# Two mask instructions a batch moved from GpSimd to VectorE, and one of them written anew

## The reference

```python
x = x + L0_xattn(layernorm(x), ctx, ctx, ...)    # autocorrelation, top 12 lags
x = x + L0_ffn(layernorm(x), ...)                # 8 experts, the best one a token
x = x + L1_xattn(layernorm(x), ctx, ctx, mask, ...)
x = x + L1_ffn(layernorm(x), ...)                # ternary weights, 8-bit activations
```

```python
k = split_heads(key @ Wk.T + bk)
scores = einsum('bhqd,bhkd->bhqk', q, k) / sqrt(16)
scores = where(mask[:, None, :, :] == 0, -1e9, scores)
p = softmax(scores, axis=-1)
```

## Time and profile before

| | us |
|---|---|
| median of 3 runs | 1647.78 |
| lowest, highest | 1644.97, 1658.26 |
| profiled execution | 1647.78 |
| its span, first to last instruction | 1645.8 |
| mean granted TensorE clock (share of full) | 0.873 |

### The profile page before, as it was taken

One profiled execution on the slowest core, in us unless ns is written; L12 is line 12 of the kernel. 1 busy time (PEld: TensorE's weight loads), 2 busy tenths in 40 slices (PEclk: granted clock), 3 DMA queues, 4 the chain that ended last, 5 costly groups with the idle time before them and its releaser, 6 DMA issues.

```text
span 1645.8 us, 31869 instructions
## 1 busy us (share of the span) xinstructions
PE 1311.1 (80%) x9726; PEld 903.2 (55%) x9726; DVE 1205.0 (73%) x3428; ACT 1010.9 (61%) x2134; POOL 732.0 (44%) x890
## 2 busy tenths in 40 slices
PE   5953354788899799889888998798888988888765
PEld 4842343555666566656665666566655655555433
DVE  4773444577888788878887888788877787777743
ACT  1311221366777677767776777677766776666664
POOL 3363433245444544455445444554444444444221
PEclk9975576698999899989998999899989999888975
DMA  7762345444444444444444444444443433332100
GB/s 275 230 215 77 115 151 167 127 132 147 144 137 133 146 140 146 134 146 137 141 143 146 137 137 140 141 149 137 128 129 114 133 122 105 108 95 85 60 8 13
DMA packets 169185, 216.96 MB, mean 132 GB/s; under 512 B 19002, under 2 KB 157628, under 8 KB 162492
## 3 DMA queue, kind: packets, MB, share of 16 engines
q1 hardware_dynamic: 162876, 198.15, 38.4%
q0 software_dynamic: 6144, 16.79, 3.2%
HBM read 133.33 MB, written 79.43 MB: 129 GB/s over the span
## 4 chain that ended last, share of the span: by engine, by line
DVE 33%; PE 28%; issue 16%; POOL 8%; ACT 6%; DMA 5%; SPq 2%; another core or an unknown queue 0%; DVEq 0%; POOLq 0%; ACTq 0%
DVE mx L1135 8%; DVE hq L1200 3%; DVE bn L918 3%; PE bank L1400 3%; PE bank L1369 3%; PE bank L1428 3%; PE bank L1359 3%; PE bank L1422 2%; DVE small L1186 2%; PE bank L1342 2%; DVE t L1181 2%; PE bank L1476 2%; ACT hid L901 2%; POOL xs_d L688 2%; DVE x L1105 2%
## 5 line engine op out<-in xcount | busy, mean ns | idle before, releaser
L1135 DVE TENSOR_REDUCE mx<-bank 128x2 f32<-128x512 f32 x512 | 328.7, 683 | 63.0 <-PE bank L1400 45.2
L704 POOL TENSOR_TENSOR hid<-hid,t 128x256 f32<-128x256 f32 x256 | 186.1, 727 | 393.8 <-DVE t L1181 393.5
L861 ACT ACTIVATE pt<-bank 128x512 f32<-128x512 f32 x512 | 293.6, 596 | 88.2 <-PE bank L1342 62.9
L1400 PE MATMUL bank<-ks,qs 62*128 62x256 f32 x1024 | 139.4, 350 | 103.3 <-DVE mx L1135 87.3
L1359 PE MATMUL bank<-pt,va 128*32 128x256 f32 x2048 | 183.7, 435 | 0.0
L1400 PEld LDWEIGHTS bank<-ks,qs 62*128 62x128 f32 x1024 | 94.2, 215 | 149.4 <-DVE mx L1135 108.9
L890 ACT ACTIVATE hid<-bank 128x256 f32<-128x256 f32 x256 | 97.7, 382 | 99.9 <-PE bank L1369 96.5
L1342 PE MATMUL bank<-qs,ks 64*128 64x256 f32 x1024 | 143.0, 361 | 12.0 <-ACT pt L861 9.7
L1181 DVE SCALAR_TENSOR_TENSOR t<-th,bank 128x256 f32<-128x256 f32 x256 | 105.7, 413 | 45.5 <-ACT th L896 37.0
L671 POOL TENSOR_TENSOR rs<-ve,mhalf 128x2 f32<-128x2 f32 x96 | 68.9, 718 | 150.0 <-DVE ve L924 149.8
L1369 PE MATMUL bank<-wg,xqt 128*128 128x256 bf16 x512 | 114.8, 312 | 25.7 <-ACT xqt L884 14.8
(11 more groups left out here) (204 smaller groups left out, 3041.4 us busy)
## 6 DMA issues: line engine op xcount, KB each, us to landing
ks<-ksplit_d SPq DMA_DIRECT2D x192, 128.0 KB
qs<-qsplit_d SPq DMA_DIRECT2D x192, 128.0 KB
ys_d<-ys SPq DMA_DIRECT2D x56, 256.0 KB
xs<-xs_d SPq DMA_DIRECT2D x24, 512.0 KB, 4.0
x<-in_x SPq DMA_DIRECT2D x32, 256.0 KB, 3.6
va<-in_ctxT SPq DMA_DIRECT2D x32, 256.0 KB, 3.4
xl<-in_x SPq DMA_DIRECT2D x32, 256.0 KB
x_d<-xl SPq DMA_DIRECT2D x32, 256.0 KB, 3.1
```

The source lines that it names most:

```text
L704: pool.tensor_tensor(part_, part_, t1[:], ALU.mult).then_inc(hid_made, 1)
L861: act.activation(pt[:, s % 4].rearrange("p a c -> p (a c)"), cbanks[s % 2][:, :], ACT.Exp).then_inc(ex_made[s % 4], 1)
L1135: dve.tensor_reduce(mx[:, t, r * H // 2 + 2 * g:r * H // 2 + 2 * g + 2], shared[:].rearrange("p (h s) -> p h s", h=2), AX_X, ALU.max).then ...
L1400: ins = pe.matmul(shared_bank(job, r)[:, j * S:(j + 1) * S], qs[par][rows, 2 * g + j, t * P:(t + 1) * P], ks[par][rows, 2 * g + j, :], sta ...
```

## The change

POOL's job `mask` is gone. DVE makes `m01` in its job `mask`: one `tensor_scalar`, `mk != 0`, after the load, after `kf_made` and after `mb_made` of the batch before (since `mbias` is now made from `m01`). DVE makes `mbias` in its job `k_split`, from rows 96 and 97 of `m01`: `(m01 - 1) * big`, with `big` the old constants with the other sign; it waits for `m01_made` and, as before, for `ks_ld` of the batch before. The tables are as they were, so DVE takes `mask` at tick `BACK + 162` and `k_split` at `BACK + 253`. In the queues above this is: `m01` between `max` 5 and `gate_up` 1, of the batch four further back in the pipeline; `mbias` between `tile_T` and `ln_c`, ahead of `k` of its own batch. SP's load of `mk` waits for `m01_made` of the batch before instead of `mb_made`. The diff is whole:

```diff
--- before.py
+++ after.py
@@ -239,7 +239,7 @@
         tri = sb("tri", [P, P], BF16)
         onesb = sb("onesb", [P, P], BF16)
         nm_rows = sb("nm_rows", [P, 3])
-        nbig = sb("nbig", [P, 1])
+        big = sb("big", [P, 1])
         wk = sb("wk", [P, KT, D])
         wq = sb("wq", [P, KT, D])
         wv = sb("wv", [P, KT, D])
@@ -529,7 +529,7 @@
                     after(sp, vp_ready, b.ago(2))
                     sp.dma_start(ct[:, b.par], ctxT[b.n:b.n + 1].rearrange("o (k p) s -> (o p) k s", p=P))\
                         .then_inc(c_ld[b.par], 16)
-                    after(sp, mb_made, b.ago(1))
+                    after(sp, m01_made, b.ago(1))
                     sp.dma_start(mk[:], bass.AP(mask.tensor, b.n * S, [[0, P], [1, S]])).then_inc(m_ld, 16)
                 if job == "stash":
                     after(sp, x2_made, b)
@@ -612,9 +612,9 @@
                 pool.memset(iota8[:, e:e + 1], float(e))
             pool.memset(iota8[:, NE - 1:NE], float(NE - 1)).then_inc(consts, 1)
             pool.wait_ge(consts, 1)
-            pool.memset(nbig[96:98, :], -BIG_LO).then_inc(consts, 1)
+            pool.memset(big[96:98, :], BIG_LO).then_inc(consts, 1)
             pool.wait_ge(consts, 2)
-            pool.memset(nbig[96:97, :], -BIG_HI).then_inc(consts, 1)
+            pool.memset(big[96:97, :], BIG_HI).then_inc(consts, 1)
             pool.wait_ge(consts, 3)
             pool.affine_select(out=ident[:], in_=ident[:], compare_op=ALU.not_equal, fill=1.0, base=0,
                                pattern=[[-1, P]], channel_multiplier=1).then_inc(consts, 1)
@@ -706,14 +706,6 @@
                     after(pool, o_out, b)
                     after(pool, bo_added, b)
                     pool.tensor_tensor(x4[:, b.par], x4[:, b.par], x3[:, b.quad], ALU.add).then_inc(x4_made, 1)
-                if job == "mask":
-                    pool.wait_ge(m_ld, b.n * 16 + 16)
-                    after(pool, kf_made, b.ago(1))
-                    pool.tensor_scalar(m01[:], mk[:], 0, 0.5, ALU.is_equal, ALU.is_lt).then_inc(m01_made, 1)
-                    after(pool, m01_made, b)
-                    landed(pool, ks_ld, b.ago(1), 128)
-                    pool.tensor_scalar(mbias, mk[96:98], 0, nbig[96:98, 0:1], ALU.is_equal, ALU.mult).then_inc(mb_made, 1)
-                    after(pool, mb_made, b)
                 if job == "k_split":
                     after(pool, kh_made, b)
                     after(pool, kf_made, b)
@@ -1024,6 +1016,15 @@
                 if job == "xT_a":
                     after(dve, xah_made, b)
                     dve.tensor_tensor(xal[:], halves(shared), xah[:].bitcast(F32), ALU.subtract).then_inc(xal_made, 1)
+                if job == "mask":
+                    dve.wait_ge(m_ld, b.n * 16 + 16)
+                    after(dve, kf_made, b.ago(1))
+                    after(dve, mb_made, b.ago(1))
+                    dve.tensor_scalar(m01[:], mk[:], 0, None, ALU.not_equal).then_inc(m01_made, 1)
+                if job == "k_split":
+                    after(dve, m01_made, b)
+                    landed(dve, ks_ld, b.ago(1), 128)
+                    dve.tensor_scalar(mbias, m01[96:98], 1.0, big[96:98, 0:1], ALU.subtract, ALU.mult).then_inc(mb_made, 1)
                 if job == "route":
                     after(dve, rt_ready, b)
                     after(dve, relg, b.ago(1))
```

## The result

| | before | after |
|---|---|---|
| median of 9 runs each, us | 1649.98 | 1663.58 |
| lowest, highest | 1644.97, 1658.54 | 1655.32, 1666.31 |
| profiled span, us | 1645.8 | 1660.1 |
| mean granted TensorE clock | 0.873 | 0.872 |

A forecast was written before the change was run, and what follows sets the result against it. TensorE was busy 80% of the span, DVE 73%, POOL 44%, so work given to DVE counts nearly everywhere. Relief 0, `m01` 8.2 and `mbias` 2.0 us added to 1647.78 gave 1658.0 us, range 1640 to 1670 (8 in 10).

The forecast's parts named there:

- POOL's relief: POOL's queue, some 2.4 us a batch freed: gain 0, as `q_split` waits for ACT; rival that it counts, chance 0.13.
- The wait on DVE for `ks`: `mbias` on DVE waits for the previous batch's `ks` landing, taken to be past by then: cost 0.
- SP's queue: SP's load of `mk` waits for `m01_made`, an earlier event, but is needed only a batch later: 0.
- Lengths: The two new DVE instructions unblocked: 280 ns for `m01`, 341 ns for `mbias`, at most 0.76 us a batch.
- The collision: On DVE, `m01` and `mbias` wait for a running POOL elementwise instruction and end 0.17 us after it.
- The rival without a collision: `m01` on DVE is not blocked by POOL, costing about 0.1 us in 8 batches: 1649 us, chance 0.17.
- `m01`, 8.2 us: `m01` on DVE, blocked by POOL's `bo` addition, delays `gate_up` and what follows in 28 batches: 8.2 us together.
- the split: `m01`'s cost by batch: 8 at 0.65 us, 15 at 0 to 0.16 us, 5 at 0.3 to 0.5 us.
- every batch pays: Rival: TensorE is ready, so all 28 batches pay 0.65 us for `m01`: 1668 us, chance 0.20.
- the first kind: The 8 batches where DVE has no idle time to absorb blocked `m01`: 0.65 us each, 5.2 us.
- `mbias`, 2 us: `mbias` ahead of `ln_c` on DVE, blocked by L708, delays `ln_c` some 0.1 us in some 20 batches: 2 us.
- The sum: Whole kernel: 8.2 us for `m01` plus 2.0 for `mbias`, 10.2 us on 1647.78 us, giving 1658.0 us, +0.6%.

The follow-up runs named there:

- the run with the neighbour moved away: Changed kernel with POOL's `bo` addition placed behind the third `gate_up` instead of the first, `m01` staying in its place on DVE: 1648.74 us, ratio 0.9991 to the kernel before.
- The run in the quiet place: Changed kernel with `m01` 25 ticks later on DVE, ahead of the fifth `gate_up`, where POOL is idle: 1656.22 us, ratio 1.0032 to the kernel before.
- the neighbour halved: Changed kernel with POOL's `bo` addition as two instructions over 256 columns in place of one over 512: 1659.7 us, ratio 1.0007 to the kernel before.

## Why the prediction was right, point by point

**POOL's relief, 0:** right for this change. POOL stood idle before `q_split` in all 32 batches before and after. Before, 24 of these waits are put down to ACT and 8 to nothing; after, all 32 to ACT. Taking both mask instructions off POOL altogether gave 0.9996; the 7.68 us of waiting in the filling went with them and gave nothing either. In a kernel without the collisions it may be worth up to 0.4%; that is open.

**The wait on DVE for `ks`, 0, and SP's queue, 0:** right; the trace names no wait before L1023, which needs the load, nor before L1027.

**Lengths:** `m01` 280 ns taken, 281 measured at best; `mbias` 341 taken, 352 measured.

**The collision:** right in kind and in size. `m01` has a median of 897 ns (0.7 to 1.0 predicted) and ends 0.15 us after the `bo` addition (0.17), `mbias` 608 ns (0.6 to 1.3). The trace agrees with the rule from "SBUF — State Buffer", section "SBUF: two separate sides", of the Trainium skill, by which whichever of the two starts first holds the shared ports for its whole instruction, and shows the blocking for an int32 input and on 2 partitions as well. Not foreseen were the two batches in which `m01` was held through two POOL instructions. I had 28 masks meet the `bo` addition; in the trace it is 25. The rival without a collision is out by the trace, and by the run with the neighbour moved away.

**`m01`, 8.2 us:** the place was right, the split was not. I measured, in 29 batches from 360 us on, the step from the start of the `bo` addition to the end of the pair of `combine`. Before it is 3.86 to 3.93 us in 10 batches and 4.0 to 5.0 in the others, 122.4 us in sum; after, it is 4.45 to 4.54 us in 23, under 3.92 in 4, and 128.1 us in sum. So nearly every batch does take on the stretched form, as the rival "every batch pays" had it; but it costs 0.6 us only in 7 of the 10 where the step had been 3.9 us (the other 3 did not change), 0.3 to 0.7 us where it had been 4.0 to 4.2, and where it had been 4.4 to 5.0 it grew by 0.3 us at most and in some batches shrank, by up to 0.5. The term is 5.7 us, where I had 8.2 us. My remark that the first kind comes with a full clock does not hold: the clock was full from 12 us before the `bo` addition to 3 us after its start in 7 of the 10 batches at 3.9 us, and in 15 of the 19 others.

**`mbias`, 2 us:** from L708 to `k`, a batch takes 6.3 instead of 6.2 us, where no sorting lies in it. The sum, 2.2 us, is as reckoned; it comes from 0.17 us in some 15 batches and not from 0.1 us in 20.

**The sum:** 10.2 us forecast. The ratio gives 0.0062 x 1650 = 10.2 us (5.8 to 14.8), the medians differ by 13.6 us, the steady part of the profiles by 12.3 us. The two local terms make 5.7 + 2.2; what the profile shows beyond them lies in two sights that I had not priced. The way from the end of the pair to `q_split` takes 17.7 us or, in 8 of the first 20 batches, 0.4 to 1.0 us more; in the kernel before it was 0.1 to 0.9 us more in 6, so that the sum grew by 2.2 us. In each of the 8 a `max` waits for its bank, as at 877 us in the changed kernel:

```profile
877.41 1.29 DVE L1136 TENSOR_REDUCE mx<-bank 128x2 f32<-128x512 f32 x2 [0.71 <-PE bank L1401]
```

Why TensorE is late there is not shown. And the sorting steps are 3.7 us longer. Both are near what one profile resolves. So the two 10.2 agree in part by luck: `m01` was reckoned 2.5 us too dear, and what I had at nothing came in: 2 us by the ratio (10.2 less 5.7 and 2.2), 4 us by the profiles (12.3 less the same). The forecast of the time, 1658.0 us, lies 5.6 us under the median of 1663.6.

**`m01`'s own length:** I had it as part of the blocked time. The run in the quiet place shows it as a cost of its own where DVE has no idle time, about 0.2 us a batch.

## What to carry to other kernels

Before a `tensor_scalar` is moved to VectorE, look at what GpSimd runs at that moment: 0.28 us of work became 0.90 us here, and the move was paid back fully by shifting GpSimd's neighbour, at no cost. Look as well at stretched instructions that are there already (least against mean duration of one form in the groups by line): in this kernel two shifts that freed those of `combine` gave 0.7 to 0.8%. And put added work where its engine waits for another one anyway; an engine taken from 44% to 40% of the span gives nothing when its next instruction waits for a third.

## What the runs showed of the hardware

- A DVE `tensor_scalar` of 256 elements from SBUF to SBUF that starts while a GpSimd `tensor_tensor` runs ends 0.15 us after it (365.77 against 365.62; 1150.30, 0.16 us after L708), with f32 (895 ns in the median) and int32 input (897 ns) alike.
- Few partitions do not spare a DVE instruction: `mbias`, on 2, is held just as `m01` on 128: 1.15 us in place of 0.35, until L708 is over.
- DVE mostly gets its turn between two GpSimd instructions that follow each other at once: with the neighbour halved, `m01` ended 0.15 us after the first half, and the pair of halves took 1.47 us, 0.06 us more than in most batches where no `m01` cut in (1.41). It is not so always: 2 of 20 were held through both halves, and in the changed kernel 2 of 32 through `gate_up` and the `bo` addition (1.59 and 1.75 us).
